# The row-score product moved ahead of the transposed-score product in both attentions of an eight-layer kernel

## The reference

```python
# sa (B = 4, S = 1024, H = 8, dk = 16)
scores = jnp.einsum('bhsd,bhtd->bhst', q, k) / jnp.sqrt(dk)
p = jax.nn.softmax(scores, axis=-1)
att = jnp.einsum('bhst,bhtd->bhsd', p, v)
...
# ba (H = 16, hd = 8, BLOCK = 64): one step for each block of 64 keys
scores = jnp.einsum('bhqd,bhkd->bhqk', Q, K_blk) * SCALE
m_new = jnp.maximum(m, scores.max(axis=-1, keepdims=True))
corr = jnp.exp(m - m_new)
exp_scores = jnp.exp(scores - m_new)
chunk_sum = exp_scores.sum(axis=-1, keepdims=True)
l_new = chunk_sum * corr + chunk_sum
out_new = out * corr + jnp.einsum('bhqk,bhkd->bhqd', exp_scores, V_blk)
```

## Time and profile before

| | |
|---|---|
| median of 3 runs | 4131.51 us (4127.62 to 4138.81) |
| the profiled execution's own time | 4136.06 us |
| its span, first to last instruction | 4134.2 us |
| PE busy | 2298.8 us (56%) |
| DVE busy | 2572.2 us (62%) |
| ACT busy | 1302.5 us (32%) |
| POOL busy | 994.7 us (24%) |
| heads of `sa` | about 2342 to 2797 us of the span |
| heads of `ba` | about 3061 to 3924 us of the span |

### The profile page before, as it was taken

The page is one execution under the profiler, slowest core; times in us unless marked ns, Lnnn a source line. Parts: engine busy times, 40 slices in busy tenths (PEclk is TensorE's granted clock), DMA queues, the critical chain, the costliest instruction groups (busy, mean ns, idle before and its releaser), DMA issues.

```text
span 4134.2 us, 51076 instructions
## 1 busy us (share of the span) xinstructions
PE 2298.8 (56%) x13272; PEld 1219.8 (30%) x13272; DVE 2572.2 (62%) x4052; ACT 1302.5 (32%) x2663; POOL 994.7 (24%) x1347
## 2 busy tenths in 40 slices
PE   2000000000076767677674699994469899898974
PEld 1000000000044555555432244443223333333343
DVE  4998899999754222222374566654467777777544
ACT  2111000000042222221201366562146666666521
POOL 4220456565401444444001011100100000000012
PEclk8555555555576777777696799996679999999866
DMA  0001312221000000000002211100321111111000
GB/s 25 25 25 51 67 39 50 39 52 38 5 0 5 0 0 0 0 0 0 6 0 75 78 27 27 27 20 2 84 67 27 31 28 30 31 27 31 17 12 20
DMA packets 160087, 112.65 MB, mean 27 GB/s; under 512 B 101838, under 2 KB 137943, under 8 KB 157978
## 3 DMA queue, kind: packets, MB, share of 16 engines
q1 hardware_dynamic: 160026, 111.94, 11.0%
HBM read 73.54 MB, written 37.75 MB: 27 GB/s over the span
## 4 chain that ended last, share of the span: by engine, by line
PE 38%; DVE 35%; issue 9%; POOL 7%; SPq 3%; ACT 3%; DVEq 1%; DMA 1%; POOLq 0%; ACTq 0%; PEldq 0%
PE psum L1652 8%; PE psum L1664 6%; PE psum L1641 5%; DVE dn_arena L718 5%; PE psum L1676 5%; DVE dn_arena L722 5%; SPq L1578 3%; DVE dn_arena L675 3%; DVE dn_arena L731 2%; DVE dn_u L721 2%; DVE ba_blockmax L1870 2%; DVE X L1036 2%; DVE dn_arena L652 1%; DVE dn_arena L684 1%; PE psum L1182 1%
## 5 line engine op out<-in xcount | busy, mean ns | idle before, releaser
L1870 DVE TENSOR_REDUCE ba_blockmax<-psum 128x16 f32<-128x1024 f32 x512 | 608.8, 1220 | 200.2 <-PE psum L1641 196.0
L1740 ACT ACTIVATE ba_pt<-psum 128x512 f32<-128x512 f32 x1024 | 542.1, 602 | 286.4 <-PE psum L1652 286.2
L509 PE MATMUL psum<-ident,dn_arena 128*128 128x128 f32 x32 | 9.0, 436 | 828.3 <-DVEq L708 828.3
L1872 DVE TENSOR_REDUCE sa_negmax<-psum 128x1 f32<-128x1024 f32 x256 | 304.3, 1220 | 163.5 <-PE psum L1641 163.1
L1641 PE MATMUL psum<-ba_ks,ba_qs 64*128 64x512 bf16 x1024 | 363.2, 434 | 46.5 <-DMA ba_ks<-ba_kstk 31.4
L1652 PE MATMUL psum<-ba_qs,ba_ks 64*128 64x512 bf16 x1024 | 337.3, 405 | 75.7 <-DVEq L59 46.5
L612 POOL TENSOR_TENSOR dn_arena<-dn_arena 128x512 f32<-128x512 f32 x128 | 263.1, 2089 | 414.1 <-DVEq L59 414.1
L1740 ACT ACTIVATE sa_pt<-psum 128x512 f32<-128x512 f32 x512 | 268.6, 603 | 199.7 <-PE psum L1652 199.7
L1664 PE MATMUL psum<-ba_pt,ba_vh 128*32 128x512 f32 x2048 | 310.3, 682 | 0.0
L509 PEld LDWEIGHTS psum<-ident,dn_arena 128*128 128x128 f32 x32 | 5.8, 217 | 831.8 <-DVEq L708 831.8
L1641 PE MATMUL psum<-sa_ks,sa_qs 96*128 96x512 bf16 x512 | 199.7, 395 | 32.8 <-DMA sa_ks<-sa_kstk 30.4
(11 more groups left out here) (453 smaller groups left out, 4667.8 us busy)
## 6 DMA issues: line engine op xcount, KB each, us to landing
dn_arena<-dn_wkg SPq DMA_DIRECT2D x64, 384.0 KB, 7.0
ba_qs<-ba_qstk SPq DMA_DIRECT2D x128, 96.0 KB, 2.1
ba_ks<-ba_kstk SPq DMA_DIRECT2D x128, 96.0 KB, 2.2
dn_wkg<-dn_arena SPq DMA_DIRECT2D x4, 1536.0 KB, 5.8
sa_qstk<-sa_pq SPq DMA_DIRECT2D x48, 128.0 KB
sa_kstk<-sa_pk SPq DMA_DIRECT2D x48, 128.0 KB
sa_qs<-sa_qstk SPq DMA_DIRECT2D x32, 192.0 KB, 2.6
sa_ks<-sa_kstk SPq DMA_DIRECT2D x32, 192.0 KB, 2.7
```

The lines of the kernel that those rows point to most:

```text
L1740: nc.scalar.activation(pt[2 * x_ + h][:, :], bank(4 + slot), ACT.Exp, scale=SCALE).then_inc(pt_in, 1)
L1870: ins = nc.vector.tensor_reduce(blockmax[g][:, r, :], src.rearrange("p (n s) -> p n s", s=BLOCK), AXX, ALU.max, negate=True)
L1872: ins = nc.vector.tensor_reduce(negmax[g][:, r:r + 1], src, AXX, ALU.max, negate=True)
```

## The change

In each half of a tile, the row-score product is now issued first and the transposed-score product second. No instruction is added or removed, and no semaphore, bank or other engine's program changes.

```diff
@@ -1687,9 +1687,9 @@
                 if ahead and r == 0:
                     t.wait_ge(loaded[lead.c % 3], lead.third(32 * len(copies), 32 * len(copies)))
                 for h in range(2):
-                    key_scores(n, x_, h)
                     if ahead:
                         rows_scores(lead, r, h)
+                    key_scores(n, x_, h)
                 if x_ == 1 and c != 0:
                     values(n.at(-1), 3)
                 if x_ in (3, 5, 7):
```

## The result

The changed kernel takes 4109.18 us (median of 4 runs, 4103.34 to 4114.59), the kernel before on the same chip 4132.66 us. The ratio is 0.9942 with a 95% interval of 0.9923 to 0.9962: 24 us less, between 16 and 32. The prediction was 4112.5 us with a range of 4097 to 4125, and faster was its likeliest case. The time is right; of the two attentions, `sa` gave a little less than its step said and `ba` nearly five times as much.

The account below looks back on a forecast made before the run. TensorE was taken to set the pace in `sa`, and product, exponential and semaphore to bound tile pairs in `ba`. Gains of 15.9 us in `sa` and 3.1 in `ba` gave 4131.5 - 19.0 = 4112.5 us, range 4097 to 4125.

Parts of the forecast that it names:

- A: `sa`, tile 5: row score 0.22 us earlier, so `out_read` comes earlier; 29 x 0.22 = 6.4 us gained.
- B: `sa`, tile 6: one row score runs in the idle 1.02 us ahead of the `out_read` wait; 6.4 us gained.
- C: `sa`, tile 3: last transposed score, now eighth of its group, has its wait covered; 30 x 0.20 = 6.0 us gained.
- D: `sa`, tiles 0, 2, 4, 5: longer row-score weight load may cost 0.05 us each, 5.8 us; half taken, 2.9 lost.
- E: `ba`: filled gap at tile 6 buys nothing; 0.05 us over 62 heads, 3 us gained, between 17 gained and 6 lost.
- the ring: Score banks: in `ba` the fourth transposed score needs the first's bank; tile 7's last goes 1.15 us after tile 6's first.
- The first: Rival: `ba` gains some 17 us, through fewer half-clock stretches or E's best case; 4098.6 us, chance 0.12.
- The second: Rival: smaller `sa` gain, one of A, B, C left at 6.4 us, nothing in `ba`; 4125 us, chance 0.23.
- The third: Rival: `sa` falls to the half clock, 1.65 us lost per stretch, 19 of 29 heads; 4143.5 us, chance 0.08.

Follow-up runs that it names:

- tile 5 alone: Kernel before with the row score first only in tile 5 of `sa`; 4126.81 us in one execution, most `sa` heads 14.68 us instead of 14.86.
- tile 6 alone: Kernel before with the row score first only in tile 6 of `sa`; 4130.58 us in one execution, most `sa` heads 14.64 us.
- the hybrid order: Changed kernel with the transposed score first again in the first half of tiles 0, 2, 4 and 5; ratio 0.9915 to the kernel before.
- lone last score: Kernel before with the row score first only in the second half of tiles 1, 3 and 7 of `ba`; 4134.74 us in one execution.

## Why the prediction was right

**A**, 0.22 us a head: shown by tile 5 alone, 2.08 to 1.86, and by VectorE's 1.37 which moved along. **B**, 0.22: shown by tile 6 alone; in the whole change, the values of tile 7 follow the first transposed score by 1.62 (2513.70 to 2515.32) instead of 1.90. Of that 0.28, 0.22 are the score moved ahead; the rest is the spacing right behind the wait, 0.22 now and 0.24 to 0.25 before:

```profile
2516.12 1.07 PE L1664 MATMUL psum<-sa_pt,sa_vh 128*32 128x512 f32 x8
```

**C**, 0.20: 0.15 in sight, which is 0.20 less the weight load. **D**, taken at half: it is the full 0.05 at four places, of which the hybrid order gives 0.18 back. With the mean heads, `sa` gives 14.83 - 14.35 = 0.48 x 29 = 14 us against 15.9. In the profiled execution two half-clock stretches took 2.0 back (15.37 instead of 14.35 in one head, 14.78 and 14.88 in two neighbours), which leaves 12, and 11.8 are seen.

**E** failed in size: 3 us against 0.23 x 62 = 14. (Counted as in step A, 61 heads both turn an output and have row scores beside tile 5; the sums are the same to 0.2 us.) The step said right what holds a pair of tiles (1.15 before and after), and that filling the idle time buys no time by itself. It was mis-sized at two places. It set gains of 0.06 a group against losses and kept 0.05, where the short head gained 0.10. Both were there: the values follow their last score 0.03 to 0.07 closer at three places, and at the pair of tiles 0 and 1 that score comes 0.06 later, which leaves 0.01 of it. The gain is nearly whole at tile 7 alone (0.07), where the ring fixes the last score. And it priced a head at the mean clock, as if the share of long heads were given. What shows in its place: before, the long head lay above 13.65 and the short one below, and the mean stayed there; with the long head at 13.58 it no longer does. That the mean stays there is what the traces show; why it does is open. A long head costs 0.28 more than a short one before (13.48 to 13.76) and 0.20 after. Before, TensorE's row scores waited 9.2 us for VectorE in 57 heads, and after the change there is no such row:

```profile
PE psum L1652 <- DVEq L59: 40.2, 45, 0.9
PE psum L1652 <- ACT ba_pt L1740: 10.3, 55, 0.2
```

So row scores that come early keep a stretch's delay from going on to the next tiles; that this is the missing 0.08 is argued, not shown. The kernel with the lone last score, which lets row scores wait behind `out_read` as before, has long heads 0.33 dearer than its short ones, and its row scores wait 14.3 us for VectorE; that speaks for it.

**Its own signs.** The prediction named three signs of being wrong. A head of `sa` did not stay at 14.8. But the mean head of `ba` moved by 0.23 us, where 0.1 was the limit, and `sa` showed a clock of 0.99, under 1.00. By these two signs the account of `ba` and of `sa`'s clock was wrong, though the time came out.

**The rivals.** The first came in part and by its own mechanism: 14 us in `ba` of the 17 it allowed. Of these, 0.10 x 61 = 6 us are the shorter short head, and 8 are fewer and cheaper half-clock stretches. With `sa` it makes 28 us by the head lengths, 24 by the runs. The second, that one of A to C would fall away, did not. The third, half-clock stretches in `sa`, is real but rare: none in 28 heads before, two after, four when `sa` alone was changed, at 1.0 us each, not the 1.65 that I had; twelve at 1.65 would have turned the sign. Over all traces, the four with the change's full order in `sa` have eight such stretches, and the five with the order of before have one. The Trainium skill's rule (same page, "What's actually happening"), that activity releases the throttle, does not order these kernels: the changed `sa` has less idle time (TensorE busy for 386.98 of 403.81 us instead of 386.07 of 415.29) and more such stretches than before, and `ba` with a longer wait has almost none.

The hit is partly luck, since it rests on errors of both signs. Against the forecast of 19.0 us, `sa` gave 2 less by its steps and 2 less again by its two stretches, `ba` 11 more, and the profiled executions differ by 4 us the other way outside the heads: 19.0 - 4 + 11 - 4 = 22, where the spans show 21.4.

## What to carry to other kernels

On an in-order engine, put ahead of a wait what does not need it, and put last in a group the instruction that would wait anyway; both are read from one head of the trace, and each moved instruction is worth its spacing and no more, until the next holder (here the ring) takes over. At the first product behind a group that reads all 128 rows, try the one whose weight load is shorter. Where a stage mixes full-clock and half-clock rounds, count the rounds of each length before pricing a change: the mean can stand still though every short round got 0.10 us shorter or 0.16 longer, or fall by twice what a short round saved.

## What the hardware showed beyond what was expected

- With 0.16 us more idle time in each head of `ba` the granted clock was 1.00 instead of 0.92, and 57 heads took 1 us longer in all.
- A float32 matmul of the turn repeated on the same output costs 0.24 us, where the others take 2.03 / 16 = 0.13 each.
- A VectorE memset of 64 columns is 112 ns in its row and lengthened the chain by 0.02 to 0.03 us only.
- The last heads of `ba` fall to the half clock in ten of the fourteen traces, among them those of before and after: 16.68 and 16.82 us between two reciprocals. In the other four the same step took 11.79 to 12.03.
